# Router from the residual sum and unsplit f32 tokens in a one-core transformer-block kernel

## The reference, cut to what matters

```python
t = _to_tokens(x)
t = t + ffn(_ln_t(t))          # _ln_t: layer norm over the 64 features

# ffn, with N = 4096 tokens, D = 64, E = 8 experts, H = 256
logits = xt @ Wr + br                          # router
top_p, top_idx = top_k(softmax(logits), 2)
weights = top_p / top_p.sum(-1)
xn = (xt - mu) * rsqrt(var + 1e-5)             # a second norm
h  = gelu(einsum('end,edh->enh', xn * ln_g + ln_b, W1) + b1)
y  = einsum('enh,ehd->end', h, W2) + b2        # every expert, every token
out = sum of weights * y over the two chosen experts
```

## Time and profile before

| | us |
|---|---|
| median of 3 runs | 260.94 (260.77 to 261.13) |
| the profiled execution, its own time | 260.44 |
| span of the profiled execution | 258.4 |
| PE busy | 228.3 (88%) |
| DVE busy | 151.1 (58%) |
| ACT busy | 129.8 (50%) |
| POOL busy | 47.0 (18%) |
| first expert matmul | at 132.1 |
| last `down` ends on the chain | at 254.5 |

### The profile page before, as it was taken

The page is one execution under the profiler, slowest core; times in us unless marked ns, Lnnn a source line. Parts: engine busy times, 40 slices in busy tenths (PEclk is TensorE's granted clock), DMA queues, the critical chain, the costliest instruction groups (busy, mean ns, idle before and its releaser), DMA issues.

```text
span 258.4 us, 3162 instructions
## 1 busy us (share of the span) xinstructions
PE 228.3 (88%) x1206; PEld 117.9 (46%) x1206; DVE 151.1 (58%) x266; ACT 129.8 (50%) x206; POOL 47.0 (18%) x44
## 2 busy tenths in 40 slices
PE   2857699999996967978479999999999999999993
PEld 2744589848462655977333223223223332333230
DVE  0791849999797798777993424424424433443344
ACT  1246741003508064166447566567567666766670
POOL 3850095003562048003300000000000000000000
PEclk9995999999997999999759999999999999999999
DMA  6970000000000000000009315080511707062001
GB/s 232 256 196 0 3 0 4 0 0 0 3 0 1 0 0 3 0 0 3 0 22 232 85 44 128 0 203 3 134 28 42 164 0 164 0 143 63 0 0 41
DMA packets 6590, 14.18 MB, mean 55 GB/s; under 512 B 2736, under 2 KB 4144, under 8 KB 5680
## 3 DMA queue, kind: packets, MB, share of 16 engines
q1 hardware_dynamic: 6576, 13.99, 22.0%
HBM read 12.81 MB, written 1.18 MB: 54 GB/s over the span
## 4 chain that ended last, share of the span: by engine, by line
PE 79%; DVE 12%; ACT 6%; DMA 1%; issue 1%; SPq 0%; DVEq 0%
PE psum L623 24%; PE psum L638 23%; PE psum L482 6%; PE psum L454 3%; PE psum L464 3%; PE psum L422 2%; DVE place L985 2%; ACT place L673 2%; PE psum L570 2%; ACT place L667 2%; PE psum L552 2%; PE psum L395 1%; PE psum L536 1%; PE psum L445 1%; PE psum L490 1%; PE psum L561 1%
## 5 line engine op out<-in xcount | busy, mean ns | idle before, releaser
L780 ACT ACTIVATE hid<-psum,b1p 128x512 f32<-128x512 f32 x128 | 77.8, 688 | 40.5 <-PE psum L623 40.5
L1075 DVE SCALAR_TENSOR_TENSOR term<-psum,sm,wide 128x512 f32<-128x512 f32 x32 | 24.0, 751 | 71.8 <-PE psum L638 71.8
L623 PE MATMUL psum<-tok,w1s 128*128 128x512 f16 x256 | 64.8, 390 | 0.0
L638 PE MATMUL psum<-hid,w 128*64 128x512 f32 x256 | 61.8, 604 | 0.0
L623 PEld LDWEIGHTS psum<-tok,w1s 128*128 128x128 f16 x256 | 22.0, 100 | 51.4 <-ACT hid L780 27.4
L638 PEld LDWEIGHTS psum<-hid,w 128*64 128x64 f32 x256 | 15.6, 136 | 32.0 <-issue 27.0
L1080 DVE TENSOR_TENSOR x<-x,term 128x512 f32<-128x512 f32 x32 | 22.2, 692 | 1.1
L482 PE MATMUL psum<-h_pad,tap_bd 128*128 128x512 f32 x36 | 15.8, 592 | 0.0
L395 PE MATMUL psum<-c,xs 128*128 128x128 f32 x32 | 7.6, 431 | 5.6 <-DMA xs<-in_x 5.6
L907 DVE SCALAR_TENSOR_TENSOR place<-h_pad,sm,place 128x512 f32<-128x512 f32 x16 | 12.0, 752 | 0.6
L482 PEld LDWEIGHTS psum<-h_pad,tap_bd 128*128 128x128 f32 x36 | 6.7, 189 | 8.2 <-issue 8.2
(11 more groups left out here) (135 smaller groups left out, 293.4 us busy)
## 6 DMA issues: line engine op xcount, KB each, us to landing
wide<-gate_store SPq DMA_DIRECT2D x14, 512.0 KB, 6.3
xs<-in_x SPq DMA_DIRECT2D x2, 512.0 KB, 5.1
w1f<-in_W SPq DMA_DIRECT2D x2, 512.0 KB, 9.6
block_out<-x SPq DMA_DIRECT2D x4, 256.0 KB, 6.5
wide<-gate_store SPq DMA_DIRECT2D x2, 384.0 KB, 5.0
hid<-in_W1T SPq DMA_DIRECT2D x1, 512.0 KB, 10.4
w<-in_W SPq DMA_DIRECT2D x1, 512.0 KB, 12.0
c<-const SPq DMA_DIRECT2D x1, 483.5 KB, 4.2
```

The lines of the kernel that those rows point to most:

```text
L623: mm = pe.matmul(h_bank(n), w1s[:, part, e, k * P:(k + 1) * P], tok[:, pair, half, b, :], start=part == 0, stop=part == 1)
L638: mm = pe.matmul(y_bank(u)[b * H:(b + 1) * H, :], w2[:, e * KT + k, :], hid[:, u % 2, B2 * k + b, :], start=k == 0, stop=k == KT - 1)
L780: act.activation(hid[:, u % 2, t, :], h_bank(n), ACT.Gelu, bias=b1p[:, e * KT + k:e * KT + k + 1]).then_inc(gelu_ready, 1)
L1075: dve.scalar_tensor_tensor(term[:, u % 2, :], y_bank(u), b2t[:, e:e + 1], gate_b[part][:, e % (E // 2), :], ALU.add, ALU.mult).then_inc(te ...
```

## The change

Three things change, and the turns with them.

**Tokens and W1 in f32.** `high_part`, `low_part`, the second and third step on W1 (L852, L853), the f16 identity and its load are gone. `features` transposes the f32 tokens (8 transposes for a pair, into slot (p, 0)), and leaves the features of image 0 on rows 0 to 63 and those of image 1 on rows 64 to 127. A tile of `up` is now two f32 matmuls of 64 rows (those of image b) and 64 columns each (`side` 0 and 1 of the 128 hidden units), with a single term each and nothing to add up. The number of matmuls in a unit stays 8, and the banks rotate as before, with slots exchanged: `up` uses slots (0, 0), (0, 1) and (1, 0), `down` writes to slot (p, 1).

**Router from the residual sum.** `router` takes x1 itself, 8 f32 matmuls of 16 columns for a pair, and runs on PE right behind `tokens`. The centring is moved into the weights: `router_weights` (PE, once, in turn 8 behind `windows` of pair 1) multiplies the router weights with the centring matrix, and `keep_router_weights` (ACT, turn 7, ahead of `keep_xd` of pair 1) copies them. `conv_in` of pair 1 waits for this copy, because it writes to the same bank.

**DVE.** The two small operations at the end of `norm_tokens` are gone; `route` scales by s[4] instead.

```diff
-    "mix_branches": (19, 21), "inverse_over_kw": (35, 39), "high_part": (30, 33), "tokens": (36, 40),
-    "residual": (22, 24), "norm_tokens": (23, 25), "keep_tokens": (32, 34), "features": (41, 43), "low_part": (6, 7),
-    "router": (42, 44), "route": (26, 28), "gates_to_rows": (45, 141), "shares": (27, 111), "biases": (10, 10),
+    "mix_branches": (19, 21), "inverse_over_kw": (35, 39), "router_weights": (8, 8), "tokens": (36, 40),
+    "residual": (22, 24), "norm_tokens": (23, 25), "keep_tokens": (32, 34), "features": (41, 43), "keep_router_weights": (7, 7),
+    "router": (36, 40), "route": (26, 28), "gates_to_rows": (45, 141), "shares": (27, 111), "biases": (10, 10),
...
-        w1s = sb("w1s", [P, 2, E, HID], F16)
...
+        wr_bd = sb("wr_bd", [P, B2, E])
+        wr_centred = sb("wr_centred", [P, B2 * E])
...
-        tok = sb("tok", [P, PAIRS, 2, B2, TT // 2 * P], F16)
+        tok = sb("tok", [P, PAIRS, N])
...
-        h_early = [bank(slot(0, 1), 0), bank(slot(0, 1), 1), bank(slot(0, 0), 1)]
-        h_late = h_early + [bank(slot(1, 1), 0), bank(slot(1, 1), 1)]
-        y_early = [bank(slot(0, 0), 0)]
-        y_late = y_early + [bank(slot(1, 0), 0)]
+        h_early = [bank(slot(0, 0), 0), bank(slot(0, 1), 1), bank(slot(0, 0), 1)]
+        h_late = h_early + [bank(slot(1, 0), 0), bank(slot(1, 0), 1)]
+        y_early = [bank(slot(0, 1), 0)]
+        y_late = y_early + [bank(slot(1, 1), 0)]
...
-            sp.dma_start(c16[:, :], const16).then_inc(const16_in, 16)
...
+                if p:
+                    pe.wait_ge(wr_centred_ready, 1)
...
+            def router_weights(p):
+
+                if p == 0:
+                    return
+                pe.wait_ge(wr_ready, 1)
+                pe.matmul(slot(p, 1)[:, 0:B2 * E], const("centre"), wr_bd[:, :, :].rearrange("p b e -> p (b e)"),
+                          start=True, stop=True).then_inc(wr_centred_done, 1)
+
+            def router(p):
+
+                pe.wait_ge(x1_ready, 2 * (p + 1))
+                pe.wait_ge(wr_centred_ready, 1)
+                for j in range(TT):
+                    mm = pe.matmul(slot(p, 1)[:, j * B2 * E:(j + 1) * B2 * E], x1[:, p, j * P:(j + 1) * P], wr_centred[:, :],
+                                   start=True, stop=True)
+                mm.then_inc(router_done, 1)
+
...
             def features(p):
 
-                pe.wait_ge(const16_in, 16)
-                to = slot(p, 1).bitcast(F16)
                 for j in range(TT):
                     if j % 4 == 0:
-                        pe.wait_ge(parts_ready, 2 * p + j // 4 + 1)
-                    for b in range(B2):
-                        a = (j // 4 * 2 + b) * CHUNK + j % 4 * P
-                        mm = pe.transpose(to[:, a:a + P], parts[p][:, (j * 2 + b) * P:(j * 2 + b + 1) * P], ident16)
+                        pe.wait_ge(xn_ready, 2 * p + j // 4 + 1)
+                    mm = pe.transpose(slot(p, 0)[:, j * P:(j + 1) * P], xc[p][:, j * P:(j + 1) * P], ident)
...
-            def router(p):
-
-                pe.wait_ge(wr_ready, 1)
-                for j in range(TT):
-                    if j % 4 == 0:
-                        pe.wait_ge(tok_ready, 2 * p + j // 4 + 1)
-                    for b in range(B2):
-                        t = j * B2 + b
-                        for part in range(2):
-                            mm = pe.matmul(slot(p, 0)[:, t * E:(t + 1) * E], tok[:, p, j // 4, b, j % 4 * P:(j % 4 + 1) * P],
-                                           wrs[:, part * E:(part + 1) * E], start=part == 0, stop=part == 1)
-                mm.then_inc(router_done, 1)
-
             def gates_to_rows(p):
 
                 pe.wait_ge(gparts_ready, p + 1)
-                pe.transpose(slot(p, 0)[:, P:2 * P], gates[:, p].rearrange("p j b e t -> p (j b e t)"), ident).then_inc(gates_done, 1)
+                pe.transpose(slot(p, 1)[:, P:2 * P], gates[:, p].rearrange("p j b e t -> p (j b e t)"), ident).then_inc(gates_done, 1)
...
-                    for part in range(2):
-                        mm = pe.matmul(h_bank(n), w1s[:, part, e, k * P:(k + 1) * P], tok[:, pair, half, b, :],
-                                       start=part == 0, stop=part == 1)
+                    if u == 0 and t == 2:
+                        pe.wait_ge(tok_ready, 2)
+                    for side in range(2):
+                        mm = pe.matmul(h_bank(n)[rows_of(side), :], w1g[rows_of(b), e, k * P + side * H:k * P + (side + 1) * H],
+                                       tok[rows_of(b), pair, half * CHUNK:(half + 1) * CHUNK], start=True, stop=True)
                     mm.then_inc(w1_done, 1)
...
-            def high_part(p):
-                for j in range(2):
-                    act.wait_ge(xn_ready, 2 * p + j + 1)
-                    act.copy(part_of(p, 0, j), split(bank(xc[p], j), H)).then_inc(high_ready, 1)
+            def keep_router_weights(p):
+
+                if p == 0:
+                    return
+                act.wait_ge(wr_centred_done, 1)
+                act.copy(wr_centred[:, :], slot(p, 1)[:, 0:B2 * E]).then_inc(wr_centred_ready, 1)
 
             def keep_tokens(p):
                 for j in range(2):
                     act.wait_ge(tok_done, 2 * p + j + 1)
-                    act.copy(tok[:, p, j, :, :].rearrange("p b n -> p (b n)"),
-                             slot(p, 1).bitcast(F16)[:, j * N:(j + 1) * N]).then_inc(tok_ready, 1)
+                    act.copy(bank(tok[:, p, :], j), bank(slot(p, 0), j)).then_inc(tok_ready, 1)
...
-            pool.tensor_copy(wrs[:, 0:E], weight("wr")).then_inc(pool_chain, 1)
-            links[0] += 1
-            pool.wait_ge(pool_chain, links[0])
-            pool.tensor_tensor(wrs[:, E:2 * E], weight("wr"), wrs[:, 0:E], ALU.subtract).then_inc(wr_ready, 1)
+            link(pool.memset(wr_bd[:, :, :], 0.0))
+            for b in range(B2):
+                blocks = pool.tensor_copy(wr_bd[rows_of(b), b, :], weight("wr")[rows_of(b), :])
+                if b == 0:
+                    link(blocks)
+                else:
+                    blocks.then_inc(wr_ready, 1)
...
-            def low_part(p):
-
-                for j in range(2):
-                    pool.wait_ge(high_ready, 2 * p + j + 1)
-                    pool.tensor_tensor(part_of(p, 1, j), split(bank(xc[p], j), H), part_of(p, 0, j), ALU.subtract).then_inc(parts_ready, 1)
-
             def weights_of_first(p):
 
                 if p:
                     return
                 pool.wait_ge(ffn_in, 16 * 3)
                 pool.wait_ge(xt_ready, 1)
-                link(pool.tensor_tensor(w1g[:, :, :], w1f[:, :, :], lng.unsqueeze(2).broadcast_to([P, E, HID]), ALU.mult))
-                link(pool.tensor_copy(w1s[:, 0, :, :], w1g[:, :, :]))
-                pool.tensor_tensor(w1s[:, 1, :, :], w1g[:, :, :], w1s[:, 0, :, :], ALU.subtract).then_inc(w1_ready, 1)
-
-            for stage, (p,) in in_turn((weights_of_first, join, high, low_part)):
+                pool.tensor_tensor(w1g[:, :, :], w1f[:, :, :], lng.unsqueeze(2).broadcast_to([P, E, HID]), ALU.mult).then_inc(w1_ready, 1)
+
+            for stage, (p,) in in_turn((weights_of_first, join, high)):
...
-                count(dve.tensor_tensor(s[:, 8, :], s[:, 4, :], s[:, 3, :], ALU.mult))
-                dve.wait_ge(dve_chain, links[0])
-                link(dve.tensor_tensor(s[:, 10, :], s[:, 8, :], s[:, 5, :], ALU.mult))
...
-                link(dve.tensor_tensor(L[2], split(slot(p, 0)[:, 0:G * E], E), over(s[:, 10, :], E), ALU.mult))
+                link(dve.tensor_tensor(L[2], split(slot(p, 1)[:, 0:G * E], E), over(s[:, 4, :], E), ALU.mult))
```

More of the change, by code:

```diff
@@ L114, in constants @@
     out[:, CONST["small_index"]] = np.arange(E, 0, -1)[None, :]
-    return out, np.eye(P, dtype=np.float16)
+    return out
 SMALL = {}
@@ L151, in small_weights, with metaformer @@
     return out
-def metaformer(nc, x, small, W1, W1T, ln_b, W2, const32, const16, out):
+def metaformer(nc, x, small, W1, W1T, ln_b, W2, const32, out):
     ctx = ExitStack()
@@ L176, in split, with rows_of @@
             return v.rearrange("p (g h) -> p g h", h=n)
+        def rows_of(half):
+            return slice(half * H, (half + 1) * H)
         def parity(g):
@@ L236, in metaformer @@
         back = x_conv
-        parts = [x_conv[p].bitcast(F16) for p in range(PAIRS)]
         h2 = [place[4][:, p, :] for p in range(PAIRS)]
@@ L1099 @@
         "in_ln_b": a["L0_ffn_ln_b"].reshape(1, E * H), "in_W2": a["L0_ffn_W2"],
[L1100 removed]
+        "const32": constants(),
     }
```

22 lines of the change are left out of this document (8 added, 14 removed).

## The result

The changed kernel takes 279.82 us (median of 4 runs, 276.63 to 281.64) where the kernel before takes 260.97 beside it: a ratio of **1.068, interval 1.059 to 1.077**, 18.9 us more. The forecast was 277.0, within 270 to 288.

The account below looks back on a forecast made before the run. It took PE as full, with one dependence through ACT in each early unit. Terms 0.9 + 1.85 - 0.35 - 1.05 + 1.6 + 12.6 + 0.5 = 16.05 on 260.44, plus 0.5 for the median, gave 277.0 us, range 270 to 288.

Parts of the forecast that it names:

- early units, 14: Units 2 to 15, three banks: fourth tile waits for first tile's gelu, 4.75 us against 3.85; 12.6 us more.
- first two `up`: First two `up`, back to back before the first `down`, partly at low clock: 7.1 us for 5.5, +1.6.
- late units, 16: Expert units with five banks: nothing turns around, a few hundredths more for the first record; 16 x 0.03 = +0.5 us.
- router ahead of L543: First pair's router matmuls on PE, between its tokens and second pair's transposes, delay the chain to the gates; +1.85 us.
- two DVE steps, POOL beside DVE: Ahead of the gates: two small DVE steps gone, -0.35 us; DVE no longer slowed by POOL's step, -1.05 us.
- centred weights: Second pair's convolution waits, through ACT's copies, for the centred router weights; +0.9 us.
- Four quarters run together: In `up`, four quarter-array f32 records run at once: 16 records in 4 rounds of 0.43, 1.72 us, as in f16.
- only two quarters at once: Rival in `up`: 8 rounds, 3.44 us, early and late units 5.4 us, 317 us in all; chance 0.12.
- short records: Rival in `up`: a quarter record takes half the time, late units about 2.8 us, 246 us in all; chance 0.05.
- The first tile comes late: Early unit: first gelu starts 1.17 us after `up` instead of 0.70, because the first tile ends together with the second.
- clock rival: Granted clock falls to 1.2 GHz for part of the early units, 13 us more, 290 us in all; chance 0.05.
- the low stretch at the first gates: After PE's wait for the gates, the first two `up` start at granted clock 0.50; kept as before.

Follow-up runs that it names:

- keep_warm: The changed kernel with matmuls of no use put into three waits of PE; 274.15 us, ratio 1.055.
- router_late: The changed kernel with the first pair's router behind the second pair's `to_frequencies` and inverse DCT; 274.07 us, ratio 1.049.
- f32_alone: The changed kernel with f32 tokens and W1 kept, but the router again behind the normed tokens and no centred weights; 276.27 us.
- router_alone: The kernel before, f16 split kept, with only the router taken from the residual sum with centred weights; 266.16 us, ratio 1.023.
- best_f32: The changed kernel with later centred weights, five banks from unit 5 on, first pair's gates and tokens ahead of second pair's norm; 262.59 us, ratio 0.996.
- weights_later: The changed kernel with the centred router weights made in the middle of the second pair's convolution and copied behind its gelu; 276.92 us.
- best_f16: The kernel before (f16 `up`) with the router's move, later weights, five banks from unit 5 on and gates ahead of second pair's norm; 259.69 us, ratio 0.998.
- best_f16c: best_f16 with the residual sum before the gates, second pair's transposes one unit later and fillers in PE's waits; 256.32 us, ratio 0.978.
- after_again: The changed kernel itself, unaltered, run once more on another chip as a reference; 279.39 us, ratio 1.070.

## Why the prediction was right

Term by term, as the prediction has them, against the profiled execution:

| term | predicted | measured |
|---|---|---|
| early units, 14 | 14 x 0.9 = 12.6 | 14 x 0.95 = 13.3 |
| first two `up` | 1.6 | 7.21 − 5.48 = 1.73 |
| late units, 16 | 0.5 | 16 x 0.045 = 0.7 |
| router ahead of L543 | 1.85 | 6.14 − 4.45 = 1.69 |
| two DVE steps, POOL beside DVE | −0.35 − 1.05 | 14.51 − 16.03 = −1.52 |
| centred weights | 0.9 | 1.33 − 0.69 = 0.64 |
| sum of these | 16.05 | 16.5 |
| low clock in three stages ahead of the units | not in the sum | 1.60 + 1.60 + 1.62 = 4.8 |

*Four quarters run together.* Right. All four records of a round, of both tiles, lie in one line of the timeline, 0.66 us for four records of 0.64 each, and the instruction with the wait that stands between the tiles doesn't part them:

```profile
175.80 0.66 PE L624 MATMUL psum<-tok,w1g 64*64 64x512 f32 x4
```

The Trainium skill (TensorE: Matmul & The Clock Gate, Part 3) has row and column tiles working at once, with 32 x 32 tiles; by 16 records in 1.88 us the trace agrees for 64 x 64. The rivals with only two quarters at once (317 us) and with short records (246 us) fall with the late units at 3.75: they asked for 5.4 and 2.8.

*The first tile comes late.* Right, 1.18 for the predicted 1.17, and the two runs with other numbers of units on three banks show the dependence as cause. The last 0.05 of the 0.95 is the late unit's own: it has it too, with five banks.

*The first two `up`.* Right in size. keep_warm shows the part of the clock: at 1.00 they take 5.42, so the low clock costs 1.79 of the 7.21. It cost the kernel before about as much (5.48, where 16 records at 0.22 would be 3.5), so the 1.73 between the kernels is not the clock's; it is the late first tiles, as the prediction worked out tile by tile.

*The router.* The place and the size were right, from L569 on. router_late takes it back whole. That the inverse DCT behind it would run at the low clock wasn't foreseen.

*The DVE steps.* The two steps that took 0.81 beside POOL, L1019 and L1023, are L1012 and L1016 in the kernel after, and take 0.29; from the end of L551 to the gates' transpose it is 14.51 us for 16.03:

```profile
132.00 0.29 DVE L1012 TENSOR_TENSOR place<-place,sm 128x128 f32<-128x128 f32 x1
...
132.65 0.29 DVE L1016 TENSOR_TENSOR place<-place,st 128x128 f32<-128x128 f32 x1
```

The two parts of this term don't simply add up: f32_alone, which keeps the two small steps, has 15.05, and router_alone, which drops them but keeps POOL's step, 15.93.

*The centred weights.* Too dear by a quarter of a microsecond: the copy of 16 columns took 0.17 for the 0.27 that I had given it as an upper bound, and the two records of L578 overlap the end of L410.

*The clock.* This is the step that failed. The prediction had a clock rival, but only inside the units, where it stood at 1.00, and it kept the low stretch at the first gates. The clock was lost ahead of the units, where the change makes PE wait longer or puts short matmuls ahead of a wait.

The inverse DCT of the second pair (L551) stands behind 16 records of 16 columns (L586), the eight of L543 and a wait of 1.58. Eight profiled executions have this order and leave the wait empty: it took 3.65, 3.52, 3.48, 3.78, 3.63 and 3.52 us in six of them (the last is best_f32), and 2.05 in weights_later and best_f16. In the four without the router there it took 2.05 each time, though the wait is as long (1.64), and 2.05 in keep_warm and best_f16c, with the wait filled. So the router there makes the low clock likely and not certain. best_f32 and best_f16:

```profile
114.66 3.52 PE psum L552 x16
...
115.65 2.05 PE L557 MATMUL psum<-c,place 128*128 128x128 f32 x16 [1.59 <-ACT place L745]
```

The second convolution waits 2.18 us for 1.67 with the centred weights ahead of it: it was over 2.7 us in five of seven executions with that wait, and in one of six without it (best_f16c, with fillers there, left out). Those two are 3.2 us of the profiled execution.

The third 1.6 is what is left, at the second pair's `windows`, of the low clock in the first `windows` stage (L402, 3.75 us for 2.02). Here PE's idle time ahead of the stage parts the executions. It was 3.54, 3.11, 3.03, 2.71 and 2.28 us in the five where the stage was slow (3.04 to 3.75 us), and 0.48 to 2.09 in the eight where it took 2.02. In those five the stage ahead of the idle time, the second pair's L392, had run in 2.05 to 2.99 us for 3.27 to 3.79, so PE was done sooner and waited longer for DVE. All five are among the ten executions with the new router, and none among the three without it. Whether that is the change or chance isn't shown.

Without this third stretch the sum is 16.5 + 3.2 = 19.7, and the median says 18.9. The forecast of 277.0 is 2.8 short, about what the clock took at the two places that it didn't see. That 279.8 still lies in its range is in part luck: the room there was kept for other terms and for a clock that falls inside the units.

Open is what decides, from one execution to the next, whether the clock holds in the convolutions of the first 40 us. With the same work there, the gram matrices started at 33.58 in router_late and at 39.93 in after_again. Every gain or loss below some 3 us in this study is therefore read from the trace's stretches and not from a median.

## What to carry to other kernels

Matmuls that share the array keep the throughput and delay the first result: here the first of four tiles came 0.48 us later, and because its bank was needed again after two more tiles, each unit paid 0.95. Count when the first tile is ready and how many banks lie between it and its next use; two more banks brought it down to 0.05. A stage moved onto PE's path costs its own time and may cost the clock of the stage behind it, as much again: look at PE's waits on both sides of it, and fill one where a bank is free. A dependence made shorter (the router from the residual sum) brings nothing until its consumers are moved forward too; here that, with more banks and filled waits, gave 2.2% over the kernel before beside it, and how much of it the filled waits would give alone isn't known.

## What the runs showed of the hardware

- Four f32 records on the four 64 x 64 quarters of the array start together (0.66 us for four of 0.64 each), also across a wait that is already fulfilled, and 16 of them take 1.88 us, 0.47 a round with the change to another tiling in it.
- A wait of nearly the same length was followed by the low clock in six of eight executions with records of 16 columns ahead of it (1.58 us), and in none of four without them (1.64 us). In the two with matmuls of no use in that wait, the clock stayed at 1.00 and the stage behind took its 2.05 us.
- A stage of the same 16 records took 3.04 to 3.75 us after PE had been idle for 2.28 to 3.54 us, and 2.02 us after 0.48 to 2.09.
- Over the eight runs of the changed kernel the mean granted clock went from 0.939 to 0.966 and the time from 281.64 to 276.63; in best_f32, from 0.936 at 269.87 us to 0.993 at 257.15. Runs at one clock still differ: 272.45 to 275.39 us at 0.968 in router_late.
- Two DVE steps of 128 elements a row that read nothing from PSUM (L1019, L1023) took 0.81 us beside a POOL step and 0.29 without one; in the same 2.34 us, the step that reads PSUM (L1018) and the reduction (L1028) took 0.29 as ever. Without POOL's step and the two small steps the path was 1.5 us shorter.
